# The block without attention ahead of the attention in one pass of the step loop, one load of the Exp table, and the residual added inside the last step

## The chip, the cores and the metric

One core of a Trainium2 chip. The metric is the device time of one execution in microseconds, as the median of several runs.

Engines by the names of the profile: PE is TensorE (PEld its weight loads, PEldq its sequencer, which carries out branches and register operations), DVE is VectorE, ACT is ScalarE, POOL is GpSimd, SP issues DMAs. Each engine runs its own stream of instructions; semaphores order them.

## The reference

Input x is 16 batches of 32 channels of 16 x 16 pixels. What is computed is a chain of blocks: a depthwise 51 x 51 convolution with normalisations; a masked attention over 256 positions with spike-gated keys, whose output is added to x; a normalisation; and then a routed network of 33 steps. The steps are what the change touches:

```python
def step(h, p):
    op = jnp.argmax(h[0, 0, :NOPS])              # 19 operations; token 0 of batch 0 chooses
    q, k, v = h @ p['wq'][op], h @ p['wk'][op], h @ p['wv'][op]
    attn = softmax(einsum('bqd,bkd->bqk', q, k) * scale)
    y = einsum('bqk,bkd->bqd', attn, v) @ p['wo'][op]
    h = where(p['am'][op], y, h)                 # attention only where the mask says so
    z = relu(h @ p['w1'][op] + p['b1'][op]) @ p['w2'][op] + p['b2'][op]
    h = where(p['fm'][op], z, h)                 # so the feed-forward block
```

The masks are such that most pairs of step and operation change nothing. The steps start from the normalised tokens; what comes out is the tokens ahead of that normalisation (the residual) plus the state after the last step.

## The kernel before

The state hT is held transposed, 128 partitions (4 batches of 32 channels) by 4 groups by 256 positions. outT holds the residual, the state ahead of the last normalisation.

**Codes.** A table made on the chip says, for each operation and step, which step is the next that does anything and of what kind: 1 feed-forward block alone, 2 attention alone, 3 both. A code of NONE (132) or more means that no step is left. Every engine keeps the code in a register and runs `While(code < NONE)`: it takes step and kind from the code (lines 777 to 782 on PE, 1036 to 1041 on ACT, 1388 to 1393 on DVE), and then passes four conditional pieces in this order: attention (`If(kind >= 2)`, line 783 on PE, 1042 on ACT, 1394 on DVE), the block without attention (`If(kind == 1)`, 864, 1078, 1444), the feed-forward block after an attention (`If(kind == 3)`, 867, 1081, 1448), and the end of an attention alone (`If(kind == 2)`, 870, 1084, 1452). Each piece is code of its own. PE's attention piece unrolls 16 batches and is much the longest. With the inputs given, three steps do something: the first is of kind 1, the second and third of kind 3.

**Feed-forward block** (`ffn`). PE first multiplies token 0 alone (829) and then, for groups 0 and 1, the state by w1 (813); token 0 goes on through ACT (1059) and PE (834, 835) to DVE, which finds the largest entry, that is the next operation opi (1157 to 1168). SP and all others wait for opi; SP then loads the next step's weights wa and wf (419, 420). ACT (1069) and DVE (1431) take two ReLUs each for either pair of groups; PE multiplies by w2 (859), two groups at a time; ACT writes hT of groups 0, 1, 2 (1075) and DVE that of group 3 (1438). If the next step attends, PE multiplies its weights by each other (772) as soon as wa has come, and DVE spreads the products into bda and bdv (1209).

**Attention's head.** PE multiplies hT by bda (512) through a ring of three banks. ACT copies the products of groups 0 and 2 to qz (1050), DVE those of 1 and 3 (1402), four copies each; the fourth product needs the bank of the first. Scores (555), row maxima on DVE (1256) and Exp on ACT (905) follow. ACT looks functions up in a table; Sqrt and Exp stand in different ones. Ahead of the loop Sqrt's is in (the normalisation). Line 1043 asks for Exp's with an operation on one element, and a further load stands ahead of the ReLU of token 0 (1059) in each feed-forward piece.

**End.** When the loop is over, DVE waits until all of hT is written (1464, 1465) and adds hT to outT in two operations of two groups each (1468); SP stores each half (434) when it is there.

Of the kernel before, what the change touches and what calls it, by code (L numbers as in the profile page):

```python
# [11 lines left out]
ALU = mybir.AluOpType  # L12
# [4 lines left out]
B, C, HW = 16, 32, 16  # L17
# [72 lines left out]
def build(nc, d):  # L90
    with ExitStack() as ctx:
# [285 lines left out]
        def _(sp):  # L377
# [206 lines left out]
        def _(pe):  # L584
# [192 lines left out]
            with pe.While(lambda: pe.snap(reg_code) < NONE):  # L777
# [5 lines left out]
                with pe.If(kind >= 2):  # L783
                    att = pe.snap(reg_att)
                    t = Tasks(LATT, pe.snap(reg_task), pe.snap(reg_da), pe.snap(reg_dd))
                    wp = pe.snap(reg_wp)
                    wait(pe, s_bd2, wp, 2)
                    pe.wait_ge(s_hlo, 2)
                    pe.wait_ge(s_hhi, 2)
                    for g in range(NG):  # L790
                        product_pe(pe, t, g, bda[:, :], hT[:, g, :], S)

                    def all_values():
                        for g in range(NG):
                            values(t, NG + g, hT, g, bdv[:, :])

                    attention_pe(pe, att, t, len(LPRE), hT, None, all_values)
# [66 lines left out]
                with pe.If(kind == 1):  # L864
                    ffn(Tasks(FF, pe.snap(reg_task), pe.snap(reg_da), pe.snap(reg_dd)), 0)
                    count_tasks(FF, False)
                with pe.If(kind == 3):
                    ffn(Tasks(LATTF, pe.snap(reg_task), pe.snap(reg_da), pe.snap(reg_dd)), K_HF, pe.snap(reg_att))
                    count_tasks(LATTF, True)
# [44 lines left out]
        def _(act):  # L914
# [119 lines left out]
            deviation(NG - 1)  # L1034

            with act.While(lambda: act.snap(reg_code) < NONE):
# [5 lines left out]
                with act.If(kind >= 2):  # L1042
                    nc.scalar.activation(table[:, :], eps[0:1, :], ACT.Exp)
                    att = act.snap(reg_att)
                    t = Tasks(LATT, act.snap(reg_task))
                    for g in range(0, NG, 2):
                        t.filled(act, g)
                        for q in range(GB):
                            rows = slice(q * C, (q + 1) * C)
                            cp = nc.scalar.activation(qz[rows, g * GB + q, :], t.bank(g)[rows, 0:S], ACT.Copy)  # L1050
                        cp.then_inc(s_da, 1)
                    attention_act(act, att, t, len(LPRE), hT, False, lambda g: copy_values(t, NG + g, g))
                    act.reg_alu(reg_att, reg_att, B, ALU.add)
# [24 lines left out]
                with act.If(kind == 1):  # L1078
                    ffn(Tasks(FF, act.snap(reg_task)), 0, False)
                    act.reg_alu(reg_task, reg_task, len(FF), ALU.add)  # L1080
                with act.If(kind == 3):
# [9 lines left out]
        def _(dve):  # L1091
# [295 lines left out]

            with dve.While(lambda: dve.snap(reg_code) < NONE):
# [5 lines left out]
                with dve.If(kind >= 2):  # L1394
                    att = dve.snap(reg_att)
                    chain["base"], chain["n"] = dve.snap(reg_c), 0
                    t = Tasks(LATT, dve.snap(reg_task))
                    for g in range(1, NG, 2):
                        t.filled(dve, g)
                        for q in range(GB):  # L1400
                            rows = slice(q * C, (q + 1) * C)
                            cp = nc.vector.tensor_copy(qz[rows, g * GB + q, :], t.bank(g)[rows, 0:S])  # L1402
                        cp.then_inc(s_dd, 1)

                    def copy_values(g):
                        t.filled(dve, NG + g)
                        nc.vector.tensor_copy(v[:, :, g * GB:(g + 1) * GB, :].rearrange("p h b c -> p h (b c)"),
                                              t.bank(NG + g)[:, 0:S].rearrange("p (h n) -> p h n", h=NH)).then_inc(s_dd, 1)

                    attention_dve(att, False, copy_values, lambda q: place_weights(q, r))  # L1410
# [9 lines left out]
                def ffn(t, k0, att=None):  # L1420
# [16 lines left out]
                    t.filled(dve, k + n)  # L1437
                    nc.vector.tensor_scalar(hT[:, n, :], bank[ZBANK[n]][:, 0:S], b2s, None, ALU.add).then_inc(s_dd, 1)
# [5 lines left out]
                with dve.If(kind == 1):  # L1444
                    chain["base"], chain["n"] = dve.snap(reg_c), 0
                    ffn(Tasks(FF, dve.snap(reg_task), dve.snap(reg_da), dve.snap(reg_dd)), 0)
                    place_next()
                with dve.If(kind == 3):
# [3 lines left out]
                with dve.If(kind == 2):  # L1452
# [73 lines left out]
```

## Time and profile before

| | us |
|---|---|
| three runs | 201.71, 201.98, 204.34 |
| median | 201.98 |
| the profiled execution: time | 200.46 |
| the profiled execution: span, first to last instruction | 198.4 |
| busy in the span: PE | 164.8 (83%) |
| DVE | 134.5 (68%) |
| ACT | 111.5 (56%) |
| POOL | 63.8 (32%) |

The loop over the steps fills the span from 97 us to 194 us; in front of it stand the convolution and the first, masked attention. PE is the busiest engine as a mean over the whole. A mean says nothing of a single stage: the busy share is over 0.9 in the attentions and far lower where the loop begins and where it ends. So what an edit is worth is read in the stretch that it touches, from what each instruction there waited for. Times in the timelines are from the start of the span; "issue" as a releaser means that nothing in the profile ended the wait.

### The profile page before, as it was taken

What the parts mean: (1) busy time and instruction counts of PE and PEld (TensorE: products, weight loads), DVE (VectorE), ACT (ScalarE), POOL (GpSimd) and SP (SyncE); (2) the same over time, 40 slices, a digit from 0 to 9 for tenths busy, and PEclk for the clock granted to TensorE, in tenths of its full rate; (3) what the DMA queues carried; (4) which work ended last, traced back from release to release, by engine and by line L of the source; (5) the groups of instructions that cost most, each with busy time, mean ns of one, the idle gap of its engine ahead of it and who ended that gap; (6) DMA issues with size and microseconds to landing.
All of it is one profiled execution on the core that took longest, in us unless ns stands there. A gap on an engine that the chain in (4) does not pass through costs nothing.

```text
span 198.4 us, 4245 instructions
## 1 busy us (share of the span) xinstructions
PE 164.8 (83%) x1252; PEld 111.7 (56%) x1256; DVE 134.5 (68%) x382; ACT 111.5 (56%) x324; POOL 63.8 (32%) x153
## 2 busy tenths in 40 slices
PE   7999988676898989879469499999687799998660
PEld 5779744232776667647233397777434687765320
DVE  1364578849947988976306589798674788888552
ACT  3464511459768655645316668666646686756640
POOL 8850000100153645444200006555500056555100
PEclk9999999996699999999966999999999999999998
DMA  5900000000000000000000000000000000000003
GB/s 140 327 11 0 3 0 3 0 3 2 0 2 0 2 0 3 0 15 5 5 3 17 5 0 0 0 0 0 0 0 15 0 0 0 0 0 0 0 3 107
DMA packets 3020, 3.33 MB, mean 17 GB/s; under 512 B 889, under 2 KB 2361, under 8 KB 3002
## 3 DMA queue, kind: packets, MB, share of 16 engines
q1 hardware_dynamic: 2858, 2.85, 4.7%
q10 hardware_dynamic: 144, 0.25, 0.3%
q8 instruction: 9, 0.15, 0.3%
q14 instruction: 9, 0.07, 0.1%
HBM read 2.58 MB, written 0.53 MB: 16 GB/s over the span
## 4 chain that ended last, share of the span: by engine, by line
PE 60%; DVE 16%; issue 10%; ACT 8%; POOL 2%; DVEq 1%; ACTq 1%; POOLq 0%
PE bank L555 17%; PE bank L528 8%; PE bank L615 5%; PE bank L542 5%; ACT qz L981 4%; PE bank L813 3%; PE bank L679 3%; PE bank L512 3%; DVE big L1269 3%; PE bank L633 3%; PE bank L859 2%; PE bank L600 2%; POOL prob L448 2%; ACT qz L1050 2%; ACT prob L905 1%
## 5 line engine op out<-in xcount | busy, mean ns | idle before, releaser
L448 POOL TENSOR_SCALAR prob<-prob,einv 128x256 f32<-128x256 f32 x96 | 44.9, 482 | 59.9 <-DVE einv L1264 59.7
L1269 DVE COPY big<-bank 128x512 f32<-128x512 f32 x48 | 32.8, 684 | 5.8 <-PE bank L528 5.8
L905 ACT ACTIVATE prob<-bank,nmax 128x256 f32<-128x256 f32 x64 | 29.8, 474 | 11.6 <-DVE nmax L1256 11.6
L528 PE MATMUL bank<-ident,prob 128*128 128x128 f32 x192 | 30.2, 280 | 6.5 <-POOL prob L448 6.4
L555 PE MATMUL bank<-hT,qz 128*128 128x256 f32 x128 | 32.7, 383 | 0.0
L528 PEld LDWEIGHTS bank<-ident,prob 128*128 128x128 f32 x192 | 21.5, 140 | 18.2 <-POOL prob L448 14.2
L1256 DVE TENSOR_REDUCE nmax<-bank 128x2 f32<-128x512 f32 x32 | 21.6, 686 | 4.8 <-PE bank L555 4.6
L555 PEld LDWEIGHTS bank<-hT,qz 128*128 128x128 f32 x128 | 22.3, 190 | 3.6 <-issue 1.6
L905 ACT ACTIVATE prob<-minus,nmax 128x256 f32<-128x256 f32 x32 | 16.0, 500 | 8.9 <-DVE nmax L1253 7.9
L555 PE MATMUL bank<-kt,qz 128*128 128x256 f32 x64 | 16.5, 386 | 0.9 <-ACT prob L905 0.9
L905 ACT ACTIVATION_READ_ACCUMULATOR prob<-bank,nmax 128x1 f32 x64 | 12.9, 202 | 0.0
L1253 DVE CUSTOM_DVE_ANT_0 minus<-bank,negm 128x256 f32<-128x256 f32 x32 | 11.9, 414 | 1.5 <-PE bank L555 1.5
L555 PEld LDWEIGHTS bank<-kt,qz 128*128 128x128 f32 x64 | 11.1, 190 | 3.2 <-ACT prob L905 1.4
L931 ACT ACTIVATE big<-bank 128x512 f32<-128x512 f32 x14 | 8.2, 598 | 8.1 <-PE bank L615 8.1
L615 PEld LDWEIGHTS bank<-ident,filt 128*128 128x128 f32 x96 | 10.8, 144 | 1.0 <-issue 0.7
L615 PE MATMUL bank<-ident,filt 128*128 128x128 f32 x96 | 11.3, 274 | 0.0
L1106 DVE COPY big<-bank 128x512 f32<-128x512 f32 x10 | 6.8, 693 | 6.6 <-PE bank L615 6.5
L1069 ACT ACTIVATE big<-bank,wfs 128x512 f32<-128x512 f32 x12 | 7.6, 684 | 6.5 <-PE bank L813 6.5
L813 PE MATMUL bank<-hT,w1r 32*128 32x512 f32 x48 | 9.8, 803 | 1.1 <-ACT hT L1065 1.1
L542 PE MATMUL bank<-big,v 128*32 128x256 f32 x160 | 10.7, 385 | 0.0
L1402 DVE COPY qz<-bank 32x256 f32<-32x256 f32 x16 | 6.7, 420 | 5.0 <-PE bank L512 4.9
L595 PE MATMUL bank<-constf,ident 128*128 128x512 bf16 x33 | 8.1, 380 | 1.0 <-DVE xc L1178 0.6
(171 smaller groups left out, 254.2 us busy)
## 6 DMA issues: line engine op xcount, KB each, us to landing
xrev<-xrev_dram SPq DMA_DIRECT2D x1, 512.0 KB, 5.2
xin<-xtok_dram SPq DMA_DIRECT2D x1, 512.0 KB, 5.7
out_dram<-outT SPq DMA_DIRECT2D x2, 256.0 KB, 2.3
maskc<-maskc_dram SPq DMA_DIRECT2D x1, 256.0 KB, 5.5
kx<-kx_dram ACTq DMA_DIRECT2D x1, 248.0 KB, 3.1
wx<-wx_dram SPq DMA_DIRECT2D x1, 216.0 KB, 4.0
constf<-constf_dram SPq DMA_DIRECT2D x1, 186.0 KB, 5.2
wa<-wa_dram SPq DMA_DIRECT2D x3, 56.0 KB, 1.7
```

Source lines behind the costliest of these rows:

```text
L448: last = nc.gpsimd.tensor_scalar(prob[b % NPB][:, ih, :], prob[b % NPB][:, ih, :], einv[:, b, ih:ih + 1], 1.0, ALU.mult, ALU.mult)
L528: mm = pe.transpose(bank[2 + b % 2][:, jh * S + ih * P:jh * S + (ih + 1) * P], prob[b % NPB][:, ih, jh * P:(jh + 1) * P], ident)
L542: mm = pe.matmul(t.bank(k0 + g)[q * C:(q + 1) * C, 0:S], v[:, jh, b, :], probT[b % NTB][:, jh, :], start=(jh == 0), stop=(jh == NH - 1), t ...
L555: mm = pe.matmul(bank[SCORES[b % AHEAD]][:, ih * S:(ih + 1) * S], qz[:, b, ih * P:(ih + 1) * P], keys[:, b // GB, :], start=True, stop=True)
L595: pe.matmul(into, ident[:, 0:P // 2].bitcast(BF16), constf[:, 0:2 * P].bitcast(BF16), start=True, stop=True)
L615: mm = pe.transpose(bank[TBANK[n]][:, u * P:(u + 1) * P], flat(filt[:, ck, a0:a0 + YH, :]), ident)
L813: pe.matmul(bank[HBANK[gp][q]][:, :], w1r[rows, :], flat(hT[rows, 2 * gp:2 * gp + 2, :]), start=True, stop=True, tile_position=(q * C, 0)) ...
L905: e = nc.scalar.activation(prob[b % NPB][:, ih, :], scores, ACT.Exp, bias=nmax[:, b, ih:ih + 1], scale=-1.0 if masked else 1.0, accum_out= ...
L931: nc.scalar.activation(dst, src, ACT.Copy).then_inc(s_toepA, 1)
L1253: m = nc.vector.tensor_tensor_reduce(minus[b % AHEAD][:, ih, :], bank[SCORES[b % AHEAD]][:, ih * S:(ih + 1) * S], negm[:, ih, :], -1.0, -F ...
L1256: m = nc.vector.tensor_reduce(nmax[:, b, :], bank[SCORES[b % AHEAD]][:, :].rearrange("p (h j) -> p h j", h=NH), AX.X, ALU.max, negate=True)
L1269: nc.vector.tensor_copy(flat(probT[b % NTB]), bank[2 + b % 2][:, :]).then_inc(s_PT, 1)
```

## The change

- PE, ACT and DVE now test `kind == 1` first. After that block they take step and kind anew from the code just loaded and go on, in the same pass, to `If(kind >= 2)`. The attention piece itself is the same, moved behind. SP and POOL keep their loops.
- ACT asks for Exp's table once, ahead of the loop, after the last Sqrt; line 1043 is gone.
- In a last step DVE adds the residual itself. Within `ffn`, after the next code has been read, DVE branches on it: with a step to come, as before; with none, it adds groups 0 and 1 once ACT has written them, then group 2, and forms the sum of group 3 from PE's product, bias and outT in one operation. The adds behind the loop are gone. For an empty loop and for a last step of kind 2 the two old adds stand in those places.
- SP waits for the first and third signal of four groups' sums in place of the first and second.

The diff, with the moved pieces cut:

```diff
             for i in range(2):
-                sp.wait_ge(s_fin, i + 1)
+                sp.wait_ge(s_fin, 2 * i + 1)
 ...
@@ PE
                 r = pe.snap(reg_r)
-                with pe.If(kind >= 2):
-                    att = pe.snap(reg_att)
 ...
-                    attention_pe(pe, att, t, len(LPRE), hT, None, all_values)
 ...
                 with pe.If(kind == 1):
                     ffn(Tasks(FF, pe.snap(reg_task), pe.snap(reg_da), pe.snap(reg_dd)), 0)
                     count_tasks(FF, False)
+                    pe.reg_alu(reg_step, reg_code, 2, ALU.logical_shift_right)
+                    pe.reg_alu(reg_step, reg_step, NSTEPS - 1, ALU.min)
+                    pe.reg_alu(reg_kind, reg_code, 3, ALU.bitwise_and)
+
+                b = pe.snap(reg_step, min_val=0, max_val=NSTEPS - 1)
+                kind = pe.snap(reg_kind)
+                r = pe.snap(reg_r)
+
+                with pe.If(kind >= 2):
+                    att = pe.snap(reg_att)
 ...
+                    attention_pe(pe, att, t, len(LPRE), hT, None, all_values)
                 with pe.If(kind == 3):
 ...
@@ ACT (block order as on PE)
             deviation(NG - 1)
+            nc.scalar.activation(table[:, :], eps[0:1, :], ACT.Exp)
 ...
-                with act.If(kind >= 2):
-                    nc.scalar.activation(table[:, :], eps[0:1, :], ACT.Exp)
 ...
@@ DVE (block order as on PE)
+            def add_state():
+                for i in range(2):
+                    gs = slice(2 * i, 2 * i + 2)
+                    nc.vector.tensor_tensor(outT[:, gs, :], outT[:, gs, :], hT[:, gs, :], ALU.add).then_inc(s_fin, i + 1)
+
+            with dve.If(dve.snap(reg_code) >= NONE):
+                dve.wait_ge(s_hlo, 2)
+                dve.wait_ge(s_hhi, 2)
+                add_state()
+
             with dve.While(lambda: dve.snap(reg_code) < NONE):
 ...
                     next_step(dve, b, reg_r, reg_op, reg_code)
                     n = NG - 1
-                    t.filled(dve, k + n)
-                    nc.vector.tensor_scalar(hT[:, n, :], bank[ZBANK[n]][:, 0:S], b2s, None, ALU.add).then_inc(s_dd, 1)
+                    with dve.If(dve.snap(reg_code) >= NONE):
+                        wait(dve, s_da, t.a, count("A", t.owners[:k + 2]))
+                        nc.vector.tensor_tensor(outT[:, 0:2, :], outT[:, 0:2, :], hT[:, 0:2, :], ALU.add).then_inc(s_fin, 1)
+                        wait(dve, s_da, t.a, count("A", t.owners[:k + 3]))
+                        nc.vector.tensor_tensor(outT[:, 2, :], outT[:, 2, :], hT[:, 2, :], ALU.add).then_inc(s_fin, 1)
+                        t.filled(dve, k + n)
+                        nc.vector.scalar_tensor_tensor(outT[:, n, :], bank[ZBANK[n]][:, 0:S], b2s, outT[:, n, :],
+                                                       ALU.add, ALU.add).then_inc(s_fin, 1)
+                    with dve.If(dve.snap(reg_code) < NONE):
+                        t.filled(dve, k + n)
+                        nc.vector.tensor_scalar(hT[:, n, :], bank[ZBANK[n]][:, 0:S], b2s, None, ALU.add).then_inc(s_dd, 1)
 ...
                     pick_op(r)
                     count_tasks(LATT, True)
                     next_step(dve, b, reg_r, reg_op, reg_code)
+                    with dve.If(dve.snap(reg_code) >= NONE):
+                        da = dve.snap(reg_da)
+                        dve.wait_ge(s_da, da)
+                        add_state()
                     weight_diagonals()
                     place_next()
-
-            da, dd = dve.snap(reg_da), dve.snap(reg_dd)
-            dve.wait_ge(s_da, da)
-            dve.wait_ge(s_dd, dd)
-            for i in range(2):
-                gs = slice(2 * i, 2 * i + 2)
-                nc.vector.tensor_tensor(outT[:, gs, :], outT[:, gs, :], hT[:, gs, :], ALU.add).then_inc(s_fin, 1)
```

## Rows read from the trace of the kernel before

**Rows 1.** The page's second part: granted clock in 40 slices of 4.96 us
```profile
PEclk9999999996699999999966999999999999999998
```

**Rows 2.** The chain that ended last, 94 to 113 us: start, duration, what
```profile
96.84 4.17 issue
```

**Rows 3.** Views of lines 783 and 777: count, duration ns min/median/max, first and last start
```profile
L783 PEldq COMPARE_BRANCH  x3: 67/67/3562, 96.9 to 151.2; - x3
...
L777 PEldq COMPARE_BRANCH  x4: 77/77/330, 96.4 to 192.0; - x4
```

**Rows 4.** DMA queues with any packets, 97 to 99.5 us, then 112 to 192 us
```profile
q8 instruction: 1, 0.02, 2.9%
...
q1 hardware_dynamic: 192, 0.07, 0.4%
```

**Rows 5.** Busy time by stretch: length, PE, PEld, DVE, ACT, POOL, clock, DMA share, GB/s
```profile
96.90:101.00 4.10, 0.00 (x0) 0.02 (x1) 0.40 (x1) 0.11 (x1) 0.00 (x0) 1.00 0.02 4
101.00:107.80 6.80, 6.67 (x38) 2.70 (x42) 3.55 (x9) 3.20 (x6) 0.09 (x1) 0.50 0.04 11
107.90:113.70 5.80, 3.21 (x30) 1.93 (x22) 2.65 (x7) 3.78 (x8) 0.00 (x0) 1.00 0.04 7
```

**Rows 6.** Timeline, first step: start, duration, engine, what, idle time before it
```profile
100.98 0.28 PEld L829 LDWEIGHTS bank<-hT,w1r 32*128 32x128 f32 x1 [4.54 <-issue]
...
104.68 0.14 DVE L1162 TENSOR_SCALAR opi<-top 1x1 int32<-1x1 f32 x1
104.78 2.73 DVE L1431 TENSOR_SCALAR big<-bank,wfs 128x512 f32<-128x512 f32 x4
...
108.86 0.52 PEld L772 LDWEIGHTS bank<-wa 32*128 32x128 f32 x4 [0.41 <-DMA wa<-wa_dram]
...
109.80 0.28 DVE L1209 SCALAR_TENSOR_TENSOR bdv<-bank,constf 128x128 f32<-128x128 f32 x1
...
110.73 1.53 PE L512 MATMUL bank<-hT,bda 128*128 128x256 f32 x6 [1.16 <-DVE bdv L1209]
```

**Rows 7.** Timeline, the second step's block after its attention, and the third's head
```profile
144.01 0.18 PEld L829 LDWEIGHTS bank<-hT,w1r 32*128 32x128 f32 x1 [0.17 <-issue]
...
146.46 0.14 DVE L1162 TENSOR_SCALAR opi<-top 1x1 int32<-1x1 f32 x1
...
149.65 1.07 PE L859 MATMUL bank<-big,wfs 128*32 128x256 f32 x16 [0.25 <-DVE big L1431]
...
151.58 0.28 DVE L1209 SCALAR_TENSOR_TENSOR bdv<-bank,constf 128x128 f32<-128x128 f32 x1
151.92 1.16 PEld L512 LDWEIGHTS bank<-hT,bda 128*128 128x128 f32 x6 [0.75 <-DVE bdv L1209]
```

**Rows 8.** Table loads and qz copies: view of line 1059, then the timeline
```profile
L1059 ACT ACT_TABLE_LOAD  x3: 1283/1283/1283, 95.7 to 183.4; - x3
...
110.77 1.28 ACT L1043 ACT_TABLE_LOAD   x1 [1.71 <-issue]
...
112.17 3.08 ACT L1050 ACTIVATE qz<-bank 32x256 f32<-32x256 f32 x8
...
113.74 0.70 PE L512 MATMUL bank<-hT,bda 128*128 128x256 f32 x2 [1.48 <-ACT qz L1050]
...
153.49 3.08 ACT L1050 ACTIVATE qz<-bank 32x256 f32<-32x256 f32 x8
```

**Rows 9.** Timeline, the tail of the last step
```profile
190.62 0.84 ACT L1075 ACTIVATE hT<-bank,wfs 128x256 f32<-128x256 f32 x2
...
191.68 0.47 ACT L1075 ACTIVATE hT<-bank,wfs 128x256 f32<-128x256 f32 x1 [0.22 <-PE bank L859]
192.11 0.48 DVE L1438 TENSOR_SCALAR hT<-bank,wfs 128x256 f32<-128x256 f32 x1 [1.19 <-PE bank L859]
194.28 1.29 DVE L1468 TENSOR_TENSOR outT<-outT,hT 128x512 f32<-128x512 f32 x2 [1.69 <-issue]
195.00 0.99 SPq L434 DMA_DIRECT2D out_dram<-outT  x2
```

More of the change, by code:

```diff
@@ L866, in _, with all_values @@
                     count_tasks(FF, False)
+                    pe.reg_alu(reg_step, reg_code, 2, ALU.logical_shift_right)
[6 more added lines that the diff above has]
+                    att = pe.snap(reg_att)
+                    t = Tasks(LATT, pe.snap(reg_task), pe.snap(reg_da), pe.snap(reg_dd))
+                    wp = pe.snap(reg_wp)
+                    wait(pe, s_bd2, wp, 2)
+                    pe.wait_ge(s_hlo, 2)
+                    pe.wait_ge(s_hhi, 2)
+                    for g in range(NG):
+                        product_pe(pe, t, g, bda[:, :], hT[:, g, :], S)
+                    def all_values():
+                        for g in range(NG):
+                            values(t, NG + g, hT, g, bdv[:, :])
+                    attention_pe(pe, att, t, len(LPRE), hT, None, all_values)
                 with pe.If(kind == 3):
@@ L1080, in _ @@
                     act.reg_alu(reg_task, reg_task, len(FF), ALU.add)
+                    act.reg_alu(reg_step, reg_code, 2, ALU.logical_shift_right)
+                    act.reg_alu(reg_step, reg_step, NSTEPS - 1, ALU.min)
+                    act.reg_alu(reg_kind, reg_code, 3, ALU.bitwise_and)
+                b = act.snap(reg_step, min_val=0, max_val=NSTEPS - 1)
+                kind = act.snap(reg_kind)
+                r = act.snap(reg_r)
+                with act.If(kind >= 2):
+                    att = act.snap(reg_att)
+                    t = Tasks(LATT, act.snap(reg_task))
+                    for g in range(0, NG, 2):
+                        t.filled(act, g)
+                        for q in range(GB):
+                            rows = slice(q * C, (q + 1) * C)
+                            cp = nc.scalar.activation(qz[rows, g * GB + q, :], t.bank(g)[rows, 0:S], ACT.Copy)
+                        cp.then_inc(s_da, 1)
+                    attention_act(act, att, t, len(LPRE), hT, False, lambda g: copy_values(t, NG + g, g))
+                    act.reg_alu(reg_att, reg_att, B, ALU.add)
                 with act.If(kind == 3):
@@ L1393, in _ @@
                 r = dve.snap(reg_r)
[L1394 to L1410, printed above, removed]
                 def count_tasks(owners, attended):
@@ L1447, in _, with copy_values @@
                     place_next()
+                    dve.reg_alu(reg_step, reg_code, 2, ALU.logical_shift_right)
+                    dve.reg_alu(reg_step, reg_step, NSTEPS - 1, ALU.min)
+                    dve.reg_alu(reg_kind, reg_code, 3, ALU.bitwise_and)
+                b = dve.snap(reg_step, min_val=0, max_val=NSTEPS - 1)
+                kind = dve.snap(reg_kind)
+                r = dve.snap(reg_r)
+                with dve.If(kind >= 2):
+                    att = dve.snap(reg_att)
+                    chain["base"], chain["n"] = dve.snap(reg_c), 0
+                    t = Tasks(LATT, dve.snap(reg_task))
+                    for g in range(1, NG, 2):
+                        t.filled(dve, g)
+                        for q in range(GB):
+                            rows = slice(q * C, (q + 1) * C)
+                            cp = nc.vector.tensor_copy(qz[rows, g * GB + q, :], t.bank(g)[rows, 0:S])
+                        cp.then_inc(s_dd, 1)
+                    def copy_values(g):
+                        t.filled(dve, NG + g)
+                        nc.vector.tensor_copy(v[:, :, g * GB:(g + 1) * GB, :].rearrange("p h b c -> p h (b c)"),
+                                              t.bank(NG + g)[:, 0:S].rearrange("p (h n) -> p h n", h=NH)).then_inc(s_dd, 1)
+                    attention_dve(att, False, copy_values, lambda q: place_weights(q, r))
                 with dve.If(kind == 3):
```

20 lines of the change are left out of this document (removed).

## Prediction

> **What bounds the kernel now.** I read the page's clock row first. Apart from two slices near 45 to 55 us, long before the change's place, and the last one, TensorE is granted less than full speed only in the two slices from 99 to 109 us [rows 1], just where the loop over the steps begins. The chain of work that ended last says why: at 96.84 us it holds 4.17 us of "issue" [rows 2], time in which nothing the profile shows was being waited for. The view by line resolves it. The branch of line 783, which skips the attention block, ran three times, twice in 67 ns and once, at 96.9 us, in 3562 ns [rows 3]. In that gap the queue that loads instructions moves one packet [rows 4]. So the first block without attention starts late because its code lies behind the whole attention block and was not there when the branch jumped to it. The same view of line 777, the loop's own test, shows 77 ns as the usual case [rows 3], and from 112 to 192 us no instruction packet moves at all [rows 4]: code once loaded stays. The table by stretches then gives the aftermath: PE idle from 96.9 to 101.0, clock 0.50 (1.2 GHz) from 101.0 to 107.8, and 1.00 (2.4 GHz) again from 107.9 [rows 5]. Last, the timelines of the first step, of the second and of the tail [rows 6 to 9], where every term below is read.
>
> The three wa loads are three steps: one without attention, two with. The change reaches the first step, the hand-over to the second, the heads of both attentions, and the end. It leaves the attention bodies alone, and those hold most of the time; what it saves at a head moves the body, which PE fills almost without a gap, by as much.
>
> **Block order, first step: 3.6 us.** In the new order the branch tested first is taken into the code right behind it. 3562 ns become about 67, and one further branch is gone (0.1). The first weight load of line 829 comes 3.6 us earlier, at 97.4 instead of 100.98 [rows 6]. What it waits for is there: PE ends its last normalisation product at 96.84 [rows 2], and the rows of hT and the weights it needs were written before that. Bounds: 3.4 if a branch costs more than its median, and 0 if the stall only changes its place.
>
> **Clock: 1.25 us.** PE then rests about 0.5 us instead of 4.1, and I expect it to stay at 1.00: in the stretch from 107.9 to 113.7, busy 3.21 of 5.80 us, it did [rows 5]. What half speed costs is the distance from line 829 to the chosen operation opi: 100.98 to 104.68, 3.70 us [rows 6], against 144.01 to 146.46, 2.45 us, in the second step at full clock [rows 7]. From opi on the path is the load of wa, not PE: opi to the weight product of line 772 takes 104.68 to 108.86, 4.18 us [rows 6]. So line 772 comes 2.45 + 4.18 = 6.63 us after line 829 where it came 7.88. PE and DVE are done just before: the four ReLUs of DVE start 0.1 after opi and take 2.73 [rows 6], then the last 16 products of line 859 take 1.07 [rows 7]; 2.55 + 2.73 + 1.07 = 6.4. With that cover gone the term would shrink. Bounds 0 (the clock falls anyway) and 1.5.
>
> **No way back to the top between steps one and two: 0.55 us.** bdv is ready 1.2 us after line 772 in both passes: 109.80 + 0.28 = 110.08 [rows 6], 151.58 + 0.28 = 151.86 [rows 7]. PE took it 0.65 us later in the first and 0.06 us later in the second, because in the first its sequencer was still walking through the skipped blocks and the loop test. The change replaces two skips, the jump back and the test by three register operations and one branch, so I take the 0.06. Bounds 0.2 and 0.6.
>
> **The Exp table: 0.7 and 0.6 us.** At the head of the second step ACT loads the table at 110.77 (1.28 us) and starts its qz copies at 112.17 [rows 8]. The product it copies started at 110.73 [rows 6]; a product takes 0.70 [rows 8], so without the load ACT starts at 111.43. PE's fourth product, at 113.74, waits for ACT's first four copies, DVE's second half waits for that product, and the row maxima wait behind DVE's copies: all of it moves up by 112.17 - 111.43 = 0.7. In the third step ACT starts at 153.49 [rows 8], and the same sum gives 151.92 [rows 7] + 0.70 = 152.62, so 0.87. There the new order costs something: coming from the top, PE, ACT and DVE must now skip the block without attention, one taken branch and a register read, 0.07 for the branch at best [rows 3], 0.3 as my allowance at most. I take 0.25 off: 0.6. The other loads that vanish, ahead of the ReLU of line 1059 in each step, stood in ACT's idle time and are worth nothing; the new one ahead of the loop (1.28 us and a one-element operation) takes the place of the one at 95.7 [rows 8] and is over before line 829 gives its result. Bounds for both heads together: 0.3 (the load is placed at the copies anyway) and 1.6.
>
> **The residual in the last step: 2.5 us.** Now DVE writes hT of group 3 at 192.11 to 192.59, finds its way out of the loop, and starts the first of two adds at 194.28, 1.69 us later; both end at 195.57 and the second store starts about 195.6 [rows 9]. After the change the add of groups 0 and 1 waits for ACT's second write, 190.62 + 0.84 = 191.46 [rows 9], and runs 0.69: till 192.2, when the first store leaves. The add of group 2 waits for ACT at 191.68 + 0.47 = 192.15, and runs till 192.6. Only then comes the fused operation on group 3. Its product was ready at 192.1, so the two adds delay it by about 0.5; that is the price of doing them on DVE in this place, and the store behind pays it. No row shows a fused operation of 256 columns: above the 0.28 of 128 columns [rows 6], at most twice that, near the 0.48 of line 1438 [rows 9], which reads the same bank. So the second store leaves at 193.1, not 195.6: 2.5 us. DVE's register loads for the next step and the new branch come first; they are over before 192.11 today, and I count on them being over at 191.5. Bounds: 2.0 (branches or the fused operation slower) and 2.8. The store itself, 195.6 to the span's end, stays.
>
> **Sum.** 3.6 + 1.25 + 0.55 + 0.7 + 0.6 + 2.5 = 9.2 us. The profiled execution took 200.46 us with a span of 198.4; it would have a span of 189.2 and take 191.3. The median of the runs shown is 201.98, 1.5 above that execution, so the forecast is 192.8 us.
>
> **A rule weighed against the rows.** At line 777 the branch back to the top took 77 ns [rows 3], and no code was loaded for the second way back [rows 4]. The Trainium skill (Runtime: NRT & Kernel Launch, "Instruction fetch mechanics") says that an engine holds two pages of code, that it fetches ahead only in a straight line, and that a taken branch out of this window stalls. Its second half agrees with the 3562 ns; its "two pages" does not agree with the ways back. By the rule in full, the new order would stall on its own way back, as in the first rival, and the time would be 199.8; by the rows it is 192.8.
>
> **Rivals.**
> *The loop's code is not all kept in the new order.* DVE's code grows by the adds, and the third step now enters over a skipped block. For it: the 3562 ns when code was missing [rows 3]. Against it: nothing was loaded again from 112 to 192 us though all engines went back once [rows 4]. One miss at the top and one behind the skip cost 2 x 3.5: 199.8 us, no change. The page named above would have it so.
> *Slower than before.* The same mechanism at every stretch of code of the third step on PE. The gain of 9.2 is used up at the third miss (3 x 3.5 = 10.5): 203.3 us, and 206.8 with four. It needs code to be thrown out that today's order, as long, keeps.
> *The missing code only moves.* The stall comes at another line of the first step: 3.5 us back, and 1.25 with it if PE's rest is as long: 196.3 to 197.6. Against it: from the branch on, code now runs straight through the block without attention and the attention.
> *The clock falls all the same*, for instance in the thin stretch after 102 us: 194.1, or a little more if it falls upon the attention's start.
> *The loads of the table stay.* The compiler puts them where it can't know which table is in. That it reloads at line 1059 in all three steps [rows 8], twice right behind Exp, shows that it goes by what could be, not by what is. In the new order every way into a block has Exp. If I am wrong: 192.8 + 1.3 = 194.1.
>
> **How the numbers follow.** The forecast has 0.78; the clock 0.06; the table 0.04; the moved stall 0.07; two misses 0.03; slower 0.02. About 2%, 4 us, is what a measurement of this kernel can tell from no change. Under 198 us lie the first four, 0.95; within 2% 0.03; slower 0.02. The range goes down to 190.6 (the profiled execution's 191.3 less the upper bounds' extra) and up to 196.6 (one miss comes back).
>
> **What would show it.** An "issue" gap of under 1 us ahead of line 829's products and 1.00 in every stretch after 60 us; no table load after the loop's start; ACT's first qz copy about 0.7 after PE's first product in both heads; a DVE time between the last ReLU and the last add with no 1.7 us hole; the last store 2.5 us nearer to the last product. The prediction is wrong if instruction packets appear between the first attention and the tail, or if the gap stands at a new line.

## The result, and the profile of the changed kernel

The changed kernel took 194.66 us as the median of four runs (194.58 to 197.01), the kernel before, beside it, 203.07 us (201.71 to 204.34). The ratio is 0.9615, 95% interval 0.9506 to 0.9723: faster by 3.9%. The forecast was 192.8 us, range 190.6 to 196.6. In two later comparisons the medians were 196.65 against 201.76, at the very edge of that range, and 194.68 against 201.74 (ratio 0.9609, 0.9557 to 0.9661).

The two profiled executions lie nearer to each other: spans of 198.4 and 192.6 us, 5.8 apart where the sum had 9.2. The page, its header and the rows of PE (busy, then granted clock in 40 slices of 4.8 us), against [rows 1]:

```profile
span 192.6 us, 4240 instructions
...
PE 163.9 (85%) x1255; PEld 111.2 (58%) x1256; DVE 134.2 (70%) x382; ACT 106.5 (55%) x319; POOL 63.5 (33%) x153
...
PEclk9999999997599999999999999999999999999696
```

The two slow slices at the head of the loop are gone. A new one stands near the end: slice 38, where the last step's block begins.

Timeline of the first step and the second's head, against [rows 6, 8] (line 814 was 829, 1225 was 1209, 1093 was 1050):

```profile
97.19 0.18 PEld L814 LDWEIGHTS bank<-hT,w1r 32*128 32x128 f32 x1 [0.89 <-issue]
...
99.64 0.14 DVE L1178 TENSOR_SCALAR opi<-top 1x1 int32<-1x1 f32 x1
...
101.48 0.32 SPq L419 DMA_DIRECT2D wa<-wa_dram  x1
...
104.59 0.52 PEld L772 LDWEIGHTS bank<-wa 32*128 32x128 f32 x4 [1.48 <-DMA wa<-wa_dram]
...
105.33 0.29 DVE L1225 SCALAR_TENSOR_TENSOR bdv<-bank,constf 128x128 f32<-128x128 f32 x1
105.68 1.16 PEld L512 LDWEIGHTS bank<-hT,bda 128*128 128x128 f32 x6 [0.57 <-DVE bdv L1225]
...
106.42 3.10 ACT L1093 ACTIVATE qz<-bank 32x256 f32<-32x256 f32 x8 [2.71 <-PE bank L512]
...
108.00 0.70 PE L512 MATMUL bank<-hT,bda 128*128 128x256 f32 x2 [0.76 <-ACT qz L1093]
```

PE's gap is down from 4.5 us to 0.9, opi comes 2.45 us after the first weight load instead of 3.70, PE takes bdv at once, and ACT starts 0.74 after PE's first product. But the product of line 772 waits for wa until 4.95 us after opi, where it was 4.18.

The tail, against [rows 9] (1448 to 1452 are the new adds, 1452 the fused one):

```profile
186.83 0.69 DVE L1448 TENSOR_TENSOR outT<-outT,hT 128x512 f32<-128x512 f32 x1 [0.58 <-ACT hT L1072]
187.01 0.47 ACT L1072 ACTIVATE hT<-bank,wfs 128x256 f32<-128x256 f32 x1 [0.22 <-PE bank L844]
187.51 0.43 DVE L1450 TENSOR_TENSOR outT<-outT,hT 128x256 f32<-128x256 f32 x1
187.55 1.21 SPq L434 DMA_DIRECT2D out_dram<-outT  x2
187.86 0.48 DVE L1452 SCALAR_TENSOR_TENSOR outT<-bank,wfs,outT 128x256 f32<-128x256 f32 x1
```

The last 16 products began at 186.30, the second store left at 188.36: 2.06 us. Before, these were 190.97 and 195.60, 4.63 us. That is 2.57 us saved, and the fused operation took 0.48. But the span ended 4.24 us after the second store's issue; before it was 2.75. The DMA view from the first store to the end shows what is new (queue, packets, MB, share; then KB per issue and us to landing), first of the changed kernel, then of the one before:

```profile
q1 hardware_dynamic: 544, 0.52, 31.6%
q8 instruction: 1, 0.02, 2.0%
q14 instruction: 1, 0.01, 0.5%
...
out_dram<-outT SPq DMA_DIRECT2D x2, 256.0 KB, 3.3
```

```profile
q1 hardware_dynamic: 544, 0.52, 46.3%
...
out_dram<-outT SPq DMA_DIRECT2D x2, 256.0 KB, 2.3
```

One packet of q8 lies among the stores. I take q8 for the queue that loads PE's code: e4_pad120 below alters PE's code alone, and only the packets of q8 change their places by it. The packet is 16 KB, began at 188.5 and took 1.60 us on one of the 16 engines; stores' packets of 1 KB take about 0.05 us. From 190.3 on the stores' packets come one after the other until 191.8, those of a single engine; all others were done by then. Before, such a packet came at 193.1, ahead of the stores. In both traces it begins 0.7 us after PE has left the loop (its exit branch ends at 187.8 here, at 192.4 before). The view of the load of wa in the first step (101 to 104.7 us) has a packet of q8 as well, begun at 102.2:

```profile
q1 hardware_dynamic: 192, 0.07, 11.9%
q8 instruction: 1, 0.02, 2.1%
q14 instruction: 1, 0.01, 1.0%
...
wa<-wa_dram SPq DMA_DIRECT2D x1, 56.0 KB, 3.1
```

And the new stretch of half clock, by stretches (length, PE, PEld, DVE, ACT, POOL, clock, DMA share, GB/s), against [rows 5]:

```profile
176.00:179.00 3.00, 1.51 (x12) 0.93 (x9) 1.55 (x3) 1.11 (x5) 1.59 (x4) 1.00 0.00 0
179.20:182.70 3.50, 3.50 (x29) 1.48 (x30) 1.49 (x7) 1.53 (x3) 0.00 (x0) 0.51 0.00 0
```

Half clock is 1.2 GHz. PE had been busy for half of the 3 us ahead of it. The block's own distance from first weight load to last 16 products went from 5.64 us to 7.24: 1.6 us.

### The profile page after: what moved, and what is told of

It is laid out like the page before. It is cut to its first block, busy times and chain, and to the rows that moved or that the text cites. A ratio compares the mean times of both kernels' runs of the same rounds, so it can differ in the third digit from the quotient of the medians.

```text
span 192.6 us, 4240 instructions
## 1 busy us (share of the span) xinstructions
PE 163.9 (85%) x1255; PEld 111.2 (58%) x1256; DVE 134.2 (70%) x382; ACT 106.5 (55%) x319; POOL 63.5 (33%) x153
## 3 DMA queue, kind: packets, MB, share of 16 engines
q1 hardware_dynamic: 2858, 2.85, 4.8%
## 4 chain that ended last, share of the span: by engine, by line
PE 61%; DVE 16%; ACT 8%; issue 7%; POOL 2%; DMA 2%; DVEq 1%; SPq 1%; POOLq 0%; ACTq 0%
PE bank L555 17%; PE bank L528 8%; PE bank L615 6%; PE bank L542 5%; ACT qz L989 4%; PE bank L798 3%; PE bank L679 3%; PE bank L512 3%; DVE big L1285 3%; PE bank L633 3%; PE bank L600 2%; POOL prob L448 2%; DMA wa<-wa_dram 2%; ACT prob L913 1%; ACT qz L1093 1%
## 5 line engine op out<-in xcount | busy, mean ns | idle before, releaser
L798 PE MATMUL bank<-hT,w1r 32*128 32x512 f32 x48 | 8.7, 711 | 1.1 <-ACT hT L1062 1.1
L595 PE MATMUL bank<-constf,ident 128*128 128x512 bf16 x36 | 8.8, 380 | 0.7 <-DVE xc L1194 0.6
L1440 DVE TENSOR_SCALAR big<-bank,wfs 128x512 f32<-128x512 f32 x12 | 8.4, 746 | 0.9 <-PE bank L798 0.9
```

The source lines that it names most:

```text
L595: pe.matmul(into, ident[:, 0:P // 2].bitcast(BF16), constf[:, 0:2 * P].bitcast(BF16), start=True, stop=True)
L798: pe.matmul(bank[HBANK[gp][q]][:, :], w1r[rows, :], flat(hT[rows, 2 * gp:2 * gp + 2, :]), start=True, stop=True, tile_position=(q * C, 0)) ...
L1440: nc.vector.tensor_scalar(relu[:, q, 2 * gp:2 * gp + 2, :], bank[HBANK[gp][q]][:, :].rearrange("p (g s) -> p g s", g=2), b1s, 0.0, ALU.add ...
```

## The experiments

Executions of one kernel differ by some us (those of the changed kernel lie between 193.2 and 198.8), and about 3 us of it arise ahead of the loop, where only e8_keep and e11_early change PE's work. So parts are read in the traces, one of each kernel, from the entrance of the loop (the end of PE's last product of line 736) to the end, taken here as the start of the last instruction, 0.05 us before the span's end. Columns: median of the runs; entrance; pause of PE there; opi after the first block's first weight load; wa's issue to line 772 in the first step; second store's issue to the end; entrance to the end. All in us. The medians come from different rounds; the kernel before, beside them, had 202.59 (e1 to e4), 201.76 (e0, e5 to e7), 201.74 (e8 to e10) and 201.31 (e11).

| kernel | median | entrance | pause | opi | wa | store | loop part |
|---|---|---|---|---|---|---|---|
| before | 203.07 | 96.8 | 4.1 | 3.70 | 2.33 | 2.70 | 101.5 |
| changed | 194.66 | 96.7 | 0.5 | 2.45 | 3.11 | 4.19 | 95.9 |
| e0_after | 196.65 | 99.9 | 0.5 | 2.46 | 2.68 | 4.31 | 94.8 |
| e10_after_again | 194.68 | 99.7 | 0.5 | 2.46 | 3.46 | 4.28 | 96.8 |
| e1_order | 199.14 | 100.1 | 0.5 | 2.46 | 2.81 | 2.70 | 98.3 |
| e2_table | 201.85 | 99.6 | 3.9 | 3.70 | 2.04 | 2.70 | 101.0 |
| e3_tail | 200.68 | 97.3 | 4.3 | 3.70 | 2.04 | 4.02 | 100.0 |
| e5_far420 | 199.91 | 96.9 | 3.9 | 3.50 | 2.04 | 2.52 | 96.6 |
| e4_pad120 | 193.27 | 100.4 | 0.6 | 2.45 | 2.03 | 2.51 | 92.1 |
| e9_pad_again | 192.31 | 100.4 | 0.6 | 2.46 | 2.04 | 2.53 | 92.0 |
| e6_spare | 195.34 | 99.6 | 0.5 | 2.46 | 3.00 | 3.75 | 94.6 |
| e7_both | 194.96 | 100.1 | 0.6 | 2.45 | 2.05 | 2.53 | 93.8 |
| e8_keep | 193.18 | 96.6 | 0.6 | 2.45 | 2.04 | 2.52 | 94.5 |
| e11_early | 190.92 | 95.9 | 0.6 | 2.46 | 2.04 | 2.52 | 92.9 |

**The parts alone.** e1_order is the changed kernel with the table request and the adds where they were:

```diff
             deviation(NG - 1)
-            nc.scalar.activation(table[:, :], eps[0:1, :], ACT.Exp)
...
                 with act.If(kind >= 2):
+                    nc.scalar.activation(table[:, :], eps[0:1, :], ACT.Exp)
```

> The new block order alone; the table is asked for in each attention as before, the residual is added behind the loop as before. My theory: the 3562 ns branch and the half-clock block after it go (3.65 + 1.25), the hand-over to the second step gains 0.75, the third step's head loses 0.3 by the extra skip, and the load of wa in the first step lands 0.7 later, because a 16 KB packet of PE's code, fetched when PE enters the next 256 instructions, now shares the DMA engines with it. In sum 4.6 us less span than before. The stores come 1.7 us after the last ReLU's work as before, so PE's exit code is fetched ahead of them and they take 2.3 us. Rival (the gain does not come from the missing code): PE's gap ahead of the first product stays over 3 us, and the time is within 1 us of before.

Pause, opi, wa and store came as written. The loop part fell by 3.2 us, not 4.6; the last step's block met half clock (1.6 us), which accounts for it. Another stretch of half clock, 3.4 us at the second step's head, cost a few tenths. Median 199.14 against 202.59 (ratio 0.972, 0.966 to 0.979).

e2_table is the kernel before with the two ACT lines of the diff above the other way round.

> The one load of the Exp table ahead of the loop alone, block order and residual as before. My theory: 0.7 us at the second step's head and 0.87 at the third's, nothing elsewhere: 1.6 us less span; the 4.2 us gap of PE and the half clock after it stay. Rival (the loads were hidden): no change beyond 0.3 us. Rival (loads stay in each block): table loads at the qz copies, no change.

PE's weight load for the first product to that for the fourth in the attention's head took 2.32 us in both heads, where it was 3.04 and 3.14 before: 0.72 and 0.82 saved. Pause and half clock stayed. The loop part fell only by 0.5, not 1.6, since a stretch of half clock came upon the second step's block (opi after 3.51 us in place of 2.45, and the products behind it another 0.54 later). Median 201.85 against 202.59, ratio 0.994 (0.989 to 1.000): the times alone don't tell it from no change, the heads in the trace do. The branch over the attention (line 783), as [rows 3]:

```profile
L783 PEldq COMPARE_BRANCH  x3: 67/67/3319, 99.7 to 154.3; - x3
```

e3_tail is the kernel before with the DVE and SP parts of the change, no moved block and no table edit.

> The residual inside the last step alone, block order and table as before. Both theories: the second store leaves 2.5 us earlier after the last product than before. They part on what the store then takes. Theory A (a 16 KB packet of PE's exit code, fetched about 1.2 us after PE's last product, holds up one DMA engine just when the stores run): an instruction packet of q8 lies among the stores' packets, the stores' landing goes from 2.3 to about 3.3 us, and the span falls only by 1.1. Theory B (the longer store of the changed kernel was chance): the landing stays at 2.3 us and the span falls by 2.5.

From the block's first weight load to the second store: 185.59 to 193.29, 7.70 us, where it was 10.27. That is 2.57 saved. And the store took 4.02 us to the end, with a q8 packet of 16 KB begun at 193.30, 0.01 us after the second store's issue. That speaks for the code packets: before, the packet came at 193.10, as early, but the stores came later. Loop part 1.5 us shorter; median 200.68 against 202.59 (0.987, 0.980 to 0.995), by itself under the 2% that can be told apart.

**Is it the distance of the jump?** e5_far420 puts code that never runs between the loop's head and the block:

```diff
+                with pe.If(kind > 4):
+                    for i in range(105):
+                        pe.matmul(bank[0][:, 0:P], ident, ident, start=True, stop=True)
                 with pe.If(kind == 1):
```

> The changed kernel with about 420 PE instructions at the head of the loop in a block that is never run, so that the block without attention again lies behind a long jump. Theory A (the 3562 ns are the fetch of code that a long jump misses): the branch takes 3.5 us again, PE stands 4 us ahead of its first product, and the first step's block runs at half clock: 4.8 us longer than the changed kernel. Rival (it was the attention's code, or its position, not the distance): no gap; within 0.5 us of the changed kernel.

The branch over the dead block (its line is 849), first execution of two:

```profile
L849 PEldq COMPARE_BRANCH  x2: 217/1777/3337, 97.0 to 149.3; - x2
```

3337 ns, PE's pause is 3.9 us, and half clock follows (101.0 to 104.4). What the new order had taken away was the long jump to code not yet there, whatever lies between; put back, it costs as much. In the third step the same jump cost 217 ns: its code was there by then. Expected were 4.8 us over the changed kernel; the medians are 3.3 apart (199.91 against e0_after's 196.65 beside it), and the traced execution, 195.62, was by 3.6 the shortest of the four. Load and store were quick here, because the dead block also moved the code packets, and that offsets part of the price. The fair comparison is with e4_pad120 below, which has them as quick: 96.6 against 92.1 for the loop part, 4.5 us.

**Do code packets hold up the loads and stores?** e4_pad120 shifts the loop's code by about 120 instructions, by a dead block of 30 products inside a branch that isn't taken anyway:

```diff
                 with pe.If(pe.snap(reg_next) != 0):
+                    if dead:
+                        with pe.If(pe.snap(reg_next) > 4):
+                            for i in range(dead):
+                                pe.matmul(bank[0][:, 0:P], ident, ident, start=True, stop=True)
```

> The changed kernel with about 120 PE instructions put ahead of the loop inside a branch that is not taken with these inputs; they shift the loop's code against the boundaries at which PE fetches code and do nothing else. Theory A (code packets hold up the load of wa and the stores): no q8 packet within the first step's load of wa nor within the stores; the weight product of line 772 starts 4.2 us after opi in place of 4.95, the store takes 2.3 to 2.8 us in place of 4.2 to the end, and the span is 2.1 us shorter than the changed kernel's. Theory B (both were chance): the packets' place changes and the two times don't; span within 0.5 of the changed kernel's. The stretch of half clock in the last step may or may not come: 1.6 us either way.

The DMA view from the stores to the end, and that of the first step's load of wa:

```profile
q1 hardware_dynamic: 544, 0.52, 44.1%
q14 instruction: 1, 0.01, 0.5%
...
out_dram<-outT SPq DMA_DIRECT2D x2, 256.0 KB, 2.2
```

```profile
q1 hardware_dynamic: 192, 0.07, 16.9%
...
wa<-wa_dram SPq DMA_DIRECT2D x1, 56.0 KB, 1.7
```

No q8 packet in either. Store 2.51 us, wa 2.03 us: the code packets held both up, and a shift of the code that changes next to nothing else (0.1 to 0.2 us at three places) takes them away. Over all traces: with a q8 packet among the stores they took 3.75 to 4.31 us (five traces of three kernels), without 2.51 to 2.70 (nine).

For wa two things must be kept apart, the landing of the load and the start of line 772. The load landed 2.64 to 3.42 us after its issue in the five traces with a q8 packet within it, 1.95 and 2.13 in the two with an 8 KB packet of q14 alone (e2_table, before), 1.72 to 1.83 in the seven with none. Line 772 started 0.04 us after the landing in the first five, 2.68 to 3.46 us after the issue. In the others it started later than that, and always 1.0 us after PE began the last 16 products of the block (e4_pad120, where these lines are 848 and 776; the load landed at 107.11):

```profile
106.40 1.07 PE L848 MATMUL bank<-big,wfs 128*32 128x256 f32 x16 [0.24 <-DVE big L1444]
...
107.40 0.52 PEld L776 LDWEIGHTS bank<-wa 32*128 32x128 f32 x4 [0.41 <-DMA wa<-wa_dram]
```

So without a q8 packet PE's own products end last there, not the load, although the view names the load; 2.03 to 2.05 is their time. That was so in the kernel before as well (landed at 108.65, line 772 at 108.86).

The loop part is 92.1 us, 2.7 to 4.7 less than in the three executions of the changed kernel. Load and store make 2.4 to 3.2 of it, half clock 0.8 to 2.0, while the shift itself costs some 0.5 us. The three executions met half clock within the loop, the two of the shifted kernel did not, and whether that is the shift's doing is not shown (e7_both, e8_keep and e11_early, shifted too, did meet it). The profiled span, 192.6 us, is no shorter than the changed kernel's, since the loop was entered at 100.4 and not at 96.7. e9_pad_again and e10_after_again are the two kernels side by side.

> The changed kernel shifted by 120 instructions, once more beside the changed kernel itself. Theory A: no code packet within the load of wa or the stores, second store to the end 2.5 us, entrance of the loop to the end 92 to 93.5 us depending on stretches of half clock, median 2 us under the changed kernel's. Theory B: median within 0.5 us of it.

> The changed kernel, unaltered, in more rounds. Theory A: a code packet of 16 KB lies among the stores' packets again, second store to the end 3.7 to 4.3 us, median 2 us over the shifted kernel's.

Medians 192.31 and 194.68 us, 2.4 apart where 2 was expected; their ratios to the kernel before were 0.951 (0.947 to 0.956) and 0.961 (0.956 to 0.966). The traces agree with the first run of each, and e0_after with them:

> The changed kernel once more, beside the next three. What is looked for is what comes back: the code packet among the stores (theory A: yes, span to the end 4.2 us after the second store's issue; theory B, chance: 2.8), and the half-clock stretch in the last step's first products (if it hangs on where TensorE's pauses fall, it may be gone: span 1.6 us shorter).

The packet among the stores came back, the half clock in the last step did not; a stretch of 3.4 us came at the second step's head (108.5) instead, one of 6.8 us in e10_after_again (108.4).

**What about the clock?** e6_spare puts two and four spare products ahead of the last two transposes of each looped attention, e7_both adds the shift.

```diff
                         for last in range(MAIN, B):
+                            if last > MAIN:
+                                spare(TOKEN0, 2 if last == MAIN + 1 else 4)
                             turn_pe(pe, att, last)
```

> The changed kernel with two and four short spare products of PE into a free bank while it waits for the last two batches of either attention (they are extra work and feed nothing). Theory C (TensorE's pauses of about 0.5 and 1 us there are what lets the clock fall in the last step): the clock is full through the last step, opi comes 2.45 us after the first weight load of the block in place of 3.5, and the span is up to 1.6 us shorter than the changed kernel's. Rival (the fall comes from the pauses earlier or is chance): half clock there as often as without. Cost if the spare products are in the way: at most 0.3 us per attention.

> The shift by 120 instructions and the spare products together. If theories A and C hold: 2.1 + 1.6 = 3.7 us less than the changed kernel, a span near 189; if only A, 2.1 less; if neither, the changed kernel's time.

The last step ran at full clock in both, but so it did in e0_after without them; a stretch of half clock came at 108.2 in one and at 149.9 in the other, at an attention's head. e7_both has a quick first load and quick stores, but its span was 194.0, not the 189 expected, and its loop part 1.7 us longer than e4_pad120's: 1.0 by the stretch of half clock, and 0.7 because the spare products had moved PE's code once more, so that a q8 packet fell into the second step's load of wa (3.07 us to line 772, where e4_pad120 has 2.37). So these two runs neither bear out nor refute that a rest of PE ahead is what brings the half clock on. e8_keep and e11_early put spare products where PE had rested longest, ahead of the loop (e8_keep at the loop's heads too), and keep a dead block (30 and 18 products, some 120 and 72 instructions) for the shift of the code:

```diff
+            spare(SPAREB, 4)
...
             for g in range(NG):
+                if g == 3:
+                    spare(SPAREB, 5)
                 product_pe(pe, st, K_Q + g, bdq[:, :], xt[:, g, :], S)
             for g in range(NG):
+                if g < 3:
+                    spare(SPAREB, 5)
                 product_pe(
```

> The shift by 120 instructions, and short spare products of PE (0.21 us each, into a free bank, feeding nothing) wherever PE rests long and the clock was seen to fall: 4 ahead of the spike product and 5 ahead of each of four products that wait for ACT's qz copies in the part before the loop, and 2 and 3 at either attention's head. Theory C (a thin PE is what lets the clock fall): full clock from the first attention's products to the tail, the loop entered at or before 96 us in place of 96.7 to 100.4, and the executions of this kernel lie within 1 us of each other; median about 190. Rival (the stretches of half clock come whatever PE does): same stretches, the entrance still between 96.7 and 100.4, and the median not under the shifted kernel's 193.3.

> The changed kernel with the spare products ahead of the loop only (4, and 5 before each of four products), and a dead block of 72 PE instructions, so that with the 48 of the spare products the loop's code lies exactly where the shift by 120 put it. Expected by theories A and C: loop entered at about 96.6 us, no code packet within the step loads of wa nor the stores, entrance to the end 92 us, in sum a span of 188.7 and a median of 190.8. If the clock falls at another place instead (rival), the entrance is 96.6 and the loop part 93 to 94: median 192 or more, no better than the shift alone.

By stretches ahead of the loop (columns as above), for e10_after_again and then e11_early:

```profile
38.00:48.00 10.00, 6.68 (x23) 2.84 (x21) 4.62 (x10) 4.51 (x10) 0.00 (x0) 0.83 0.01 2
48.00:58.00 10.00, 7.67 (x28) 6.11 (x29) 8.21 (x20) 7.39 (x18) 2.38 (x6) 0.66 0.00 1
```

```profile
38.00:48.00 10.00, 9.43 (x41) 4.60 (x41) 6.10 (x14) 6.39 (x14) 0.00 (x0) 1.00 0.01 2
48.00:58.00 10.00, 9.38 (x53) 6.82 (x53) 7.96 (x22) 7.74 (x17) 3.60 (x8) 1.00 0.00 1
```

With PE kept busy for 9.4 of 10 us the clock stayed at 1.00, and the loop was entered at 95.9 us in place of 99.7. Over all traces the entrance goes with the half clock between 39 and 59 us: one stretch of 6.8 us in the four entered at 96.7 to 97.3, two (3.4 and 6.8) in the eight entered at 99.6 to 100.4, none in e8_keep and e11_early (96.6 and 95.9). So ahead of the loop the rests of PE do bring the half clock on, and it makes about 3 us of the scatter. e11_early's six runs lie between 189.89 and 191.25 us; the seven of the shifted kernel without spare products, e9_pad_again, from 191.55 to 194.67, the seven of the changed kernel, e10_after_again, from 193.22 to 198.75. (The kernel before scattered in e11_early's round as in the others, from 199.85 to 203.79.)

Inside the loop it is not settled: 3.4 us of half clock came all the same, at 146.8 in e8_keep and 145.1 in e11_early. e8_keep missed what was expected of it: a median of 193.18 in place of about 190, level with the shifted kernel's 193.3 in e4_pad120 and above its 192.31 beside it, and runs from 190.36 to 194.4, not within 1 us. Its trace shows two prices. The spare products at the third step's head stood in the way at half clock: PE's first to fourth product took 3.48 us there, where half clock alone made it 2.85 (e11_early, e7_both) and full clock 2.33. And they had moved PE's code, so that, as in e7_both, a q8 packet fell into the second step's load of wa (3.15 us to line 772).

e11_early is the fastest: 190.92 us against 201.31, ratio 0.949 (0.944 to 0.954), with a span of 188.8 us. That the median met the expected 190.8 is in part luck: the entrance was 0.7 us earlier than written, the loop part 0.9 longer.

## Why the prediction was right, and where its steps were off

Direction, size and range held. Term by term, from the profiled pair (before minus after; the loop was entered 0.14 us earlier):

| step | forecast | measured |
|---|---|---|
| missing code at the long jump | 3.6 | 3.65 |
| first block at full clock | 1.25 | 1.25 |
| from opi to line 772 | 0 | -0.77 |
| from line 772 to PE's first product | 0.55 | 0.75 |
| table, second step's head | 0.7 | 0.72 |
| third step's head in all | 0.6 | 0.48 |
| clock in the last step | 0 | -1.60 |
| second store earlier | 2.5 | 2.57 |
| the store's own time | 0 | -1.49 |

**Block order.** Right in mechanism and size; e1_order and e5_far420 show it from both sides. The hand-over gained 0.2 more than written, since bda no longer waits behind DVE's write of hT, which ends earlier than wa comes.

**Load of wa.** The step "opi to the weight product takes 4.18 us" failed. The sum kept a distance from the trace of before, although the change moves what else is on the DMA engines. In its place: a packet of PE's code within the load, 2.64 to 3.42 us to the landing where it is 1.72 to 1.83 without any. The reading under it was off too: "the path is the load of wa, not PE" does not hold in the profile before, where line 772 came 0.21 us after the landing and right behind PE's own products. With the first block at full clock and no code packet, opi to line 772 is 3.88 us (e4_pad120), not 4.18.

**"The store itself stays"** failed for the same reason: it took 1.0 to 1.6 us more than before, in e3_tail as well (1.3), where nothing but the adds was moved. The profile before did show the packet, at 193.1 us, 1.9 us ahead of the first store; the change brings the stores 2.6 us forward, just upon it.

**Clock.** Full clock in the first block was right in every trace of the new order but e5_far420, which has the long jump. That it would stay full everywhere was not, and "1.00 in every stretch after 60 us" among the signs failed: in most traces one stretch of 3.4 us or more comes within the loop, in one two, at changing places (the head of the second or the third step, the last block), 0.3 to 2.0 us each. The other executions of the kernel before were at half clock for longer than its profiled one, wherever it fell: that one had a mean clock of 0.961 and was with 200.46 us among its shortest, most others had 0.938 to 0.949 and 201 to 204 us.

**Table.** 0.7 and 0.82 (e2_table) against 0.7 and 0.87. The extra skip cost 0.35 us, not 0.25: the 0.07 us of a branch behind the allowance was read where the branch doesn't jump (the 67 ns passes of line 783 went on into the attention), and this one jumps (213 ns). In the third step's head PE's sequencer is now later than bdv (the chain of waits):

```profile
145.87 0.25 DVE bdv L1225
146.12 0.41 issue
```

**Why the total fits nevertheless.** By luck, in good part. Three losses that were not in the sum make 3.9 us (0.77 + 1.60 + 1.49); the measured column adds up to 5.6, and with 0.14 at the entrance that is the 5.8 between the two spans but for rounding, where the sum had 9.2. But the sum was taken off the median, 201.98, and the medians differ by 8.4 (5.1 and 7.1 in later rounds), since the profiled execution of before was one of its shortest and that of after a usual one. Had the two profiles alone been compared, the forecast of 189.2 for the span would have missed by 3.4 us. The ends of the range are rough as well: the lower one is taken off the profiled execution and the upper one off the median, and by their own terms they come to 190.4 and 196.3, not 190.6 and 196.6.

**The rivals.** Missing code moved elsewhere: no. Code thrown out: no, no long branch in any trace of the new order but the one made on purpose in e5_far420. "The clock falls all the same" did come true, though at another place, the last block, for 1.60 us. One sign of being wrong showed and meant nothing: packets of q8 did appear between the first attention and the tail, at 102.2, 121.7 and 138.7, because the loop's code is now loaded in another order. They are as many as before (nine in the whole), none is in the third step before the exit, no branch stalled, and of the transfers only the load of wa in the first step was held up. The Trainium skill's "two pages" for code (Runtime: NRT & Kernel Launch, "Instruction fetch mechanics") is not borne out by PE: in the kernel before and in the changed one the third step runs through all of the loop's code again without a packet of q8 up to the exit, although that code had come in four of them; in e5_far420 the way back crosses 420 instructions more, and nothing stalled. The same section also gives PE room for 128 KiB of code, eight blocks, and that fits. Its blocks of 16 KB and its stall at a jump to code not yet there are borne out (nine packets of q8, 0.15 MB; 3.3 to 3.7 us).

## What to carry to other kernels

Code that is jumped over can cost as if it were far away: the piece that runs first belongs right behind the test. Here the price of getting it wrong was 3.3 to 3.7 us, once, at the first jump to code not yet there, with the clock's fall behind it. A load or store on the critical path has the code packets for company, so when an edit moves either, look in the trace for which instruction packets lie within the transfer, before and after; a hundred or so dead instructions moved them out here, and any further edit of PE's code can move one back in. Where a view names a load as what ended a wait, compare the time of its landing: if it is not right ahead of the start, something else ended last. And compare profiles only with their own execution's place among the runs in mind.

## What was new about the hardware

- One 16 KB code packet takes 0.9 to 1.7 us on one DMA engine, and the last packets of a 256 KB store wait behind it: 2.5 to 2.7 us to the end become 3.75 to 4.3. A 56 KB load landed after 1.7 to 1.8 us without one and after 2.6 to 3.4 with one.
- A jump of PE to code not yet loaded took 3319 to 3727 ns in four traces; the same jump later, with the code there, took 217 ns (e5_far420), and in the third step of the kernel before and the changed one no code was loaded again before the exit.
- TensorE's half clock ahead of the loop made about 3 us of scatter between executions, and was gone when short spare products filled PE's rests there (190.92 us, runs within 1.4 us of each other).
